# A second plain unit for expert 0, other places for two sets of weight maxima, and a reordered opening in a fused AdaLN, scan and mixture-of-experts kernel

## The reference, cut to what matters

```python
mod = (silu(c) @ wmod).reshape(4, 6, 1, 512)          # six rows of 512 for each batch
sa, ca, ga, sb, cb, gb = (mod[:, i] for i in range(6)) # ga, gb kept away from 0
h = layernorm(x) * (1 + ca) + sa
xn = rmsnorm(h) * gamma
q, kv, a = split(xn @ w_qkva.T)                        # 512 columns each
s[t] = sigmoid(a[t]) * s[t - 1] + kv[t]                # a scan over the tokens
x = x + ga * (q * s)
h = layernorm(x) * (1 + cb) + sb
p = softmax(h @ Wr); the two best experts of each token; at most 320 rows per expert and batch
y = relu(rows @ W1[e] + b1[e]) @ W2[e] + b2[e]
x = x + gb * (sum over the two experts of p * y)
```

## Time and profile before

| what | us |
|---|---|
| median of 3 runs | 2270.05 (2268.99 to 2272.29) |
| the profiled execution, its time | 2275.81 |
| its span, first to last instruction | 2274.0 |
| PE busy | 2172.6 (96%) |
| DVE busy | 1634.9 (72%) |
| ACT busy | 1042.0 (46%) |

### The profile page before, as it was taken

One profiled execution on the slowest core, in us unless ns is written; L12 is line 12 of the kernel. 1 busy time (PEld: TensorE's weight loads), 2 busy tenths in 40 slices (PEclk: granted clock), 3 DMA queues, 4 the chain that ended last, 5 costly groups with the idle time before them and its releaser, 6 DMA issues.

```text
span 2274.0 us, 34385 instructions
## 1 busy us (share of the span) xinstructions
PE 2172.6 (96%) x12890; PEld 1194.3 (53%) x12890; DVE 1634.9 (72%) x2864; ACT 1042.0 (46%) x2051; POOL 362.8 (16%) x334
## 2 busy tenths in 40 slices
PE   4899999999996889999999999999999999999997
PEld 1345455555463455564646556465555646556463
DVE  6398898898785778758758775875876687587441
ACT  4256676575443254434615534362552535255150
POOL 1014334334232101000010110101011010100101
PEclk7999999999998999999999999999999999999999
DMA  7759999576663534533544453454445355343201
GB/s 239 221 160 240 234 257 204 140 194 135 145 191 79 153 116 125 147 79 94 143 115 100 128 146 76 113 143 95 121 107 140 84 116 145 88 116 94 42 6 24
DMA packets 353064, 300.99 MB, mean 132 GB/s; under 512 B 242459, under 2 KB 242459, under 8 KB 352384
## 3 DMA queue, kind: packets, MB, share of 16 engines
q1 hardware_dynamic: 331136, 256.63, 41.2%
q0 software_dynamic: 21760, 42.14, 9.9%
HBM read 163.84 MB, written 93.01 MB: 113 GB/s over the span
## 4 chain that ended last, share of the span: by engine, by line
PE 86%; DVE 5%; DMA 3%; issue 2%; SPq 2%; ACT 1%; POOL 0%; another core or an unknown queue 0%; DVEq 0%; POOLq 0%; ACTq 0%
PE bank L1964 34%; PE bank L1907 28%; PE bank L1819 20%; DMA reg_d<-in_w 2%; PE bank L1896 1%; PE bank L1774 1%; PE bank L1741 1%; PE bank L1785 1%; DMA reg_e<-reg_e 1%; SPq L484 1%; SPq L476 1%; DVE wm L1481 0%; PE bank L1734 0%; DMA reg_d<-in_wmod 0%; DVE reg_e L1522 0%
## 5 line engine op out<-in xcount | busy, mean ns | idle before, releaser
L1964 PE MATMUL bank<-reg_b,reg_c 128*128 128x512 f16 x3840 | 833.6, 379 | 18.2 <-DVE reg_e L1442 17.2
L1964 PEld LDWEIGHTS bank<-reg_b,reg_c 128*128 128x128 f16 x3840 | 375.8, 98 | 470.8 <-DVE reg_e L1442 18.6
L1819 PE MATMUL bank<-reg_c 128*128 128x512 f16 x2304 | 511.4, 381 | 11.5 <-DMA reg_c<-reg_a 11.5
L1907 PE MATMUL bank<-reg_e,reg_a 128*128 128x320 f16 x2880 | 450.2, 300 | 8.1 <-DVE reg_e L1513 4.5
L1819 PEld LDWEIGHTS bank<-reg_c 128*128 128x128 f16 x2304 | 223.7, 98 | 274.9 <-issue 20.1
L1907 PEld LDWEIGHTS bank<-reg_e,reg_a 128*128 128x128 f16 x2880 | 281.7, 98 | 122.8 <-DVE reg_e L1513 4.8
L731 POOL DMA_INDIRECT out_dram<-reg_e,midx x80 | 139.9, 1749 | 1044.1 <-DVE reg_e L1446 933.0
L940 ACT ACTIVATE reg_e<-bank,b1s 128x320 f32<-128x320 f32 x120 | 63.2, 527 | 410.0 <-PE bank L1907 410.0
L1907 PE MATMUL bank<-reg_e,reg_d 128*128 128x320 f16 x1440 | 234.7, 301 | 8.2 <-DVE reg_e L1536 8.2
L1442 DVE SCALAR_TENSOR_TENSOR reg_e<-bank,inv,reg_e 128x512 f32<-128x512 f32 x80 | 59.8, 748 | 241.8 <-PE bank L1964 241.8
L1907 PEld LDWEIGHTS bank<-reg_e,reg_d 128*128 128x128 f16 x1440 | 140.3, 98 | 68.0 <-DVE reg_e L1536 9.2
(11 more groups left out here) (227 smaller groups left out, 2600.3 us busy)
## 6 DMA issues: line engine op xcount, KB each, us to landing
reg_d<-in_w SPq DMA_DIRECT2D x232, 512.0 KB, 4.4
slot_rows<-zrow SPq DMA_DIRECT2D x32, 516.0 KB, 5.1
reg_b<-in_x SPq DMA_DIRECT2D x16, 1024.0 KB, 7.6
out_dram<-reg_b SPq DMA_DIRECT2D x16, 1024.0 KB, 7.3
reg_d<-in_w SPq DMA_DIRECT2D x8, 1024.0 KB, 8.8
slot_rows<-zrow SPq DMA_DIRECT2D x32, 129.0 KB, 5.0
reg_d<-in_wmod SPq DMA_DIRECT2D x4, 1024.0 KB, 14.4
reg_e<-mod_rows SPq DMA_DIRECT2D x7, 512.0 KB, 9.6
```

Source lines behind the costliest of these rows:

```text
L1819: ins = mm(dst[:, :], wqs[:, ws, kc, e0:e0 + P], xns[:, j % 2, xs, kc, :], start=kc == 0 and xs == 0 and ws == 0, stop=kc == KC - 1 and ws ...
L1907: ins = mm(dst[:, 0:CAP], w[ws][:, c, p * P:(p + 1) * P], xs_of[:, KC * xs + 2 * i + c, j * CAP:(j + 1) * CAP], start=first and c == 0 and ...
L1964: ins = mm(bank_y[i % 2][:, :], hid[:, hs, hc, t * P:(t + 1) * P], w2s[:, ws, hc, :], start=k == 0 and hs == 0 and ws == 0, stop=k == HC - ...
```

## The change

1. **Unit 1 is plain too** (`PLAIN = 2`). `first_unit` becomes `plain_unit(u)` and runs for v = 0 and 1; pairs are counted from unit 2 on (`pairs_to`). The sums of expert 0 on DVE and ACT, their eight fills, and `x_sums`, `x_hi`, `x_lo` of unit 1 are gone.
2. **Maxima of expert 1.** The fills of its `w1` for the maxima stand first in the order of the fills, the first four of them ahead of SP's wait for the scattered rows. DVE takes the eight maxima of `w1` at t = 0 and t = 3 of unit 0's outputs, and those of `w2` in the plain unit 1, after every third lo part from i = 6 on. POOL's `all_max(1, 0)` moves to tile 3 of unit 0.
3. **Opening.** `wmod` piece 1 is loaded and spread ahead of piece 0. PE makes all six batch rows ahead of the first attention product, row 5 in bank 1. DVE takes two of the four maxima of `wq` between the two halves of `apply1`. SP issues the transposes of block 0 before the loads of blocks 2 and 3. The loads of expert 0's `w1` move behind the transposes of block 1, and its maxima to the end of step 1 and the middle of step 2, with their scale.

```diff
-MOD_BANK = {0: 6, 1: 5, 2: 2, 3: 3, 4: 4, 5: 5}
+MOD_BANK = {0: 6, 1: 5, 2: 2, 3: 3, 4: 4, 5: 1}
+MOD_DONE = {1: 1, 0: 2, 2: 5, 3: 6, 4: 7, 5: 8}
...
+        def pairs_to(v):
+            return NP * (v - PLAIN)
...
# sync
+            load_wmod(1)
             load_wmod(0)
-            load_wmod(1)
...
-            sp.wait_ge(s_modmm, 5)
-            load_x(0, 2)
...
             turn_x(0, 0)
+            sp.wait_ge(s_modmm, MOD_DONE[5])
+            load_x(0, 2)
+            load_x(0, 3)
...
                 if has(i, 1):
                     turn_x(*rel(q, j, 1))
+                if i == 0:
+                    for c in range(4):
+                        sp.dma_start(stage[:, c, :], w1[0, c * P:(c + 1) * P, :]).then_inc(s_stg[c], 16)
+                    sp.dma_start(b1r[:, :], b1[0, :, :]).then_inc(s_b1, 16)
...
                 load_gb()
+                bring_w1(1, fill_max(1, 0), 0)
                 for k in range(2):
                     sp.wait_ge(s_send[k], 16 * 2 * TB * NB // 2)
                 sp.wait_ge(s_xt, 16)
                 load_unit(1, 1)
-                bring_w1(0, fill_w1(0), 0)
-                bring_w1(0, fill_w1(0), 1)
...
# scalar
             square(0)
             hi1(0)
+            mod_copy(0)
+            mod_copy(1)
             act.wait_ge(s_wch0, WQ_LINKS - 4)
...
-                    if u == 0 and e == 0:
-                        sums_hi(0, 0)
-                    if v + 1 < 2 * E:
+                    if PLAIN <= v + 1 < 2 * E:
                         x_hi(v + 1)
...
# vector
             apply1(0, 0, 0)
+            wq_max(0)
+            wq_max(1)
+            apply1(0, 0, 1)
+            wq_max(2)
+            wq_max(3)
...
                 if i == 1:
                     scales_done()
-                    for c in (0, 1):
+                if i == 2:
+                    for c in (2, 3):
                         w_max_quarter(0, 0, c)
                     w_scale_head(0, 0)
...
-                    for c in (2, 3):
+                if i == 1:
+                    for c in (0, 1):
                         w_max_quarter(0, 0, c)
...
+                    elif i >= W2_NEXT and i % 3 == 0 and (i - W2_NEXT) // 3 < 8:
+                        max_piece(1, 1, (i - W2_NEXT) // 3)
...
                 if u == 0 and e == 0:
                     if t == 0:
-                        sums(0, 0)
...
                         for k in range(4):
                             max_piece(1, 0, k)
+                    if t == 3:
+                        for k in range(4, 8):
+                            max_piece(1, 0, k)
+                        scale_head(1, 0)
+                    if t == 4:
+                        scale_tail(1, 0)
...
# tensor
+            mod_spread(1)
             mod_spread(0)
-            mod_spread(1)
+            mod_mm(0)
+            mod_mm(1)
...
-            for m in range(2, 5):
+            for m in range(2, 6):
+                if m == 5:
+                    pe.wait_ge(s_modc, 1)
                 mod_mm(m)
...
-                if n == 0 and c == 0 and kind == 2:
-                    pe.wait_ge(s_modc2, 3)
+                if n == 0 and c == 0 and kind == 1:
+                    pe.wait_ge(s_modc2, 6)
...
             for v in range(2 * E):
-                if v == 0:
-                    first_unit()
+                if v < PLAIN:
+                    plain_unit(v)
```

More of the change, by code:

```diff
@@ L63 @@
 NLINK = 12
+PLAIN = 2
+W2_NEXT = 6
 EXPONENT = 0x7F800000
@@ L572, in next_unit @@
             def next_unit(v):
-                wait(sp, s_p3, NP * (v - 1))
+                if v == PLAIN:
+                    sp.wait_ge(s_mm1, 2 * HC * PLAIN)
+                wait(sp, s_p3, pairs_to(v))
                 wait_alone(sp, s_meta, v - 1)
@@ L867, in step @@
                     sigmoid(n, 2)
-                    if i == 0:
-                        for m in (5, 0, 1):
-                            mod_copy(m)
                     sigmoid(n, 3)
@@ L919, in first_unit @@
                     hb, b = i // 2, i % 2
-                    wait(act, s_mm1, i + 1)
-                    wait(act, s_hlo, i + 1)
-                    bias = b1s[:, b, hb:hb + 1]
+                    wait(act, s_mm1, 2 * HC * u + i + 1)
+                    wait(act, s_hlo, 2 * HC * u + i + 1)
+                    bias = b1s[:, 2 * u + b, hb:hb + 1]
                     src = bank_h[i % 4][:, 0:CAP]
@@ L985, in blocks_hi @@
             def blocks_hi(e, f):
-                wait(act, s_p3, NP * (2 * e - 1))
+                if 2 * e == PLAIN:
+                    act.wait_ge(s_mm1, 2 * HC * PLAIN)
+                wait(act, s_p3, pairs_to(2 * e))
                 wait(act, s_nch, NLINK * (e - 1) + 7)
@@ L1151, in _, with wq_max @@
             apply1(0, 0, 0)
-            apply1(0, 0, 1)
-            for c in range(KC):
+            def wq_max(c):
                 dve.wait_ge(s_wqraw[c], 16)
@@ L1409, in b1_scale @@
             def b1_scale(e):
-                wait(dve, s_h21, NP * (2 * e - 1))
+                if e > 0 and 2 * e == PLAIN:
+                    dve.wait_ge(s_hhi, 2 * HC * PLAIN + 4)
+                wait(dve, s_h21, pairs_to(2 * e))
                 for b in range(B):
@@ L1589, in x_sums @@
                 wait(dve, s_xt, 16 * (v + 1))
-                wait(dve, s_p3, NP * (v - 1))
-                wait(dve, s_l12, NP * (v - 1))
+                if v == PLAIN:
+                    dve.wait_ge(s_hlo, 2 * HC * PLAIN + 4)
+                wait(dve, s_p3, pairs_to(v))
+                wait(dve, s_l12, pairs_to(v))
                 v_.tensor_tensor(x32[:, :, :], x_raw[:, 0:KC, :], x_raw[:, KC:2 * KC, :], ALU.add).then_inc(s_x32, 1)
@@ L1918, in pair_step @@
                     wait(pe, s_h21, n - 2)
-                    if p % 4 == 0 and (v == 1 or v % 2 == 0):
+                    if n == 0:
+                        pe.wait_ge(s_hhi, 2 * HC * PLAIN + 4)
+                    if p % 4 == 0 and v % 2 == 0:
                         for q in range(4):
```

166 lines of the change are left out of this document (66 added, 100 removed).

## The result

The changed kernel takes 2210.98 us, the median of 4 runs (2210.73 to 2212.34), against 2270.36 us (2268.99 to 2272.29) of the kernel before: 59.4 us less, a ratio of 0.9739 with a 95% interval of 0.9722 to 0.9756. The forecast was 2210.5.

A forecast was written before the change was run, and what follows sets the result against it. PE bounds the kernel, busy 96% of the span, so gains lie in its idle time, lower clock or less work. Units 34.8 plus opening 24.8 give 59.6 us: 2270.05 - 59.6 = 2210.5 us, range 2203 to 2222.

The forecast's parts named there:

- Unit 0's second layer: Experts: with earlier fills, PE's 16.45 us wait before the third tile goes; the layer ends at 750.9.
- The cover: Unit 0's second layer: tile 0 is free near 713, PE needs it at 719.8, so 7 us of lateness cost nothing.
- The 8.8 us of landing: Unit 0's first four fills: time from first issue to the end of the DMA wait, so they land at about 706.1.
- Unit 1's first layer: Experts: 384 matmuls at 0.1358 us take 52.2 us against 68.0, no wait; second layer starts 34.8 us sooner.
- The rivals in the units: Fills pace unit 1: 2226 us, chance 0.07; clock drops in plain unit: 2215, 0.04; unit 2 starves: 2282, 0.02.
- Opening: Up to the first attention product: PE starts it at 47.2 instead of 59.16, bounds 44 and 50.
- Step 1: Starts at 82.4 instead of 105.1, held by block 1's transposes behind the zero fills; takes 33.0 us instead of 41.0.
- My 11.5: Block 1's transposes before step 1: time from first issue until the last was needed and there, in the kernel before.
- Steps 2 and 3: Attention steps that receive the moved maxima, 4.48 us twice: 77 us together instead of 71.1, bounds 70 and 80.1.
- everything hidden: Lower bound of steps 2 and 3, 70 us; as a rival, DVE hides the moved maxima: 2200 us, chance 0.11.
- the 5.20 us wait: Kernel before: PE's wait for DVE at step 1's start, with 4.48 us of maxima ahead of it on DVE.
- The base: Time the 59.6 us gain is taken from: the median 2270.05 us, not the profiled 2275.81; profiled span expected near 2214.

The follow-up runs named there:

- the eighth experiment: Changed kernel with eight more maxima of the same four quarters, 9.2 us of DVE, ahead of unit 0's first output: 2212.60 us.
- the fourth experiment: Changed kernel with the first four fills of expert 1's w1 put back behind the wait for scattered rows and the load of unit 1's rows: 2226.77 us.
- the third: Kernel before with only the first four w1 fills for the sums moved ahead of SP's wait for scattered rows; unit 1 keeps seven products: 2261.55 us.
- the second kernel: Kernel before with only the opening changed, including the moved maxima of expert 0's w1; units as before: 2245.77 us.

## Why the prediction was right

**Unit 0's second layer**: no wait at tile 2, 722.33 - 669.19 = 53.1 us, forecast 53.2 (697.7 to 750.9). The cover was 8.1 us by the eighth experiment, where 7 were forecast. The 8.8 us of landing are those of all four fills; the first was there after 4.8 in the fourth experiment. Under that cover it made no difference.

**Unit 1's first layer**: 52.2 us from start to start, forecast 52.2, and no wait for a fill. Of the 105.3 us between the second layers (forecast 105.4) the gain is 34.9, forecast 34.8. What I could not have said is how it divides; the third and fourth experiments do. My text gave the tile's wait to the place of the fills alone, but with the seven-product form that place brings less than half of what the layer lost, since the rows of unit 1 are next.

**The rivals in the units** fell: no fill paced unit 1, the granted clock was 1.00 over unit 1's first layer, its upper level of 2.4 GHz (the row below is that stretch: us, busy time and count of PE, PEld, DVE, ACT and POOL, clock, DMA share, GB/s), and unit 2 started behind unit 1's second layer with no gap, at 826.29. The Trainium skill ("TensorE: Matmul & The Clock Gate", section "A second HAM failure mode: psum-queue depth-cycling") tells of a PE that idles briefly between groups of matmuls as it goes round its banks, and so drops in and out of the lower clock. This stretch does not show it: 384 matmuls over four banks kept a pitch of 0.136 us with no idle time between them.

```profile
722.00:775.00 53.00, 53.00 (x390) 37.94 (x388) 25.37 (x43) 27.20 (x62) 1.55 (x1) 1.00 0.28 85
```

**Opening**: first product at 47.65, forecast 47.2; its terms were off in part. The four batch rows behind the maxima started at 31.56 as told, but the lower clock cost them 9.29 - 7.03 = 2.3 us, not 1.2. That price is no constant: the nine traces with this opening have from 0 to 2.5 us at this place, and the first product at 44.9 to 48.6.

Step 1 began at 81.85, forecast 82.4, with 2.24 us of wait, forecast 3.3. This term was right by luck, since two errors cancelled. The zero fills went out at 57.36, not 55.0, and the transposes at 73.58, not 71.1; but they landed 8.3 us later, not 11.3. My 11.5 (which went into the sum as 11.3) was no landing time: PE did not wait at 105.1, so the rows of before show only that the transposes were there by then. Step 1 took 114.7 - 81.85 = 32.8 us, forecast 33.0. Steps 2 and 3 took 192.1 - 114.7 = 77.4, forecast 77. In all 216.8 - 192.1 = 24.7, forecast 24.8. So close a match is chance too: with the same code, step 4 began at 214.8 to 216.8 in three traces of the old opening, and at 189.7 to 192.1 in four of the new.

**Steps 2 and 3**: with everything hidden I put them at 70, and the experiments with short and with spread maxima took 69.3 and 68.8. Between the profiled executions the 8.96 us of moved maxima cost 77.4 - 69.3 = 8.1 us, through 2.77 + 0.35 + 0.86 + 1.40 us of wait and the lower clock; between the medians they cost 6.9 us, where I charged 7. The forecast of 77 was a choice near the upper bound, by likeness to the 5.20 us wait, and not a sum of waits.

**The base**: the gain was taken from the median, not from the profiled execution, whose 2275.81 us would have given 2216. The execution shown of before had a slow first layer of unit 0 that the change does not touch. For the same reason the profiled span came out at 2210.6 us and not near 2214, as I had expected.

## What to carry to other kernels

A wait inside a chain of engines has a second-latest cause, and the gain of an edit is the distance to it: the same four fills moved forward brought 8.6 us in one form of the next layer and 15.5 in the other. A simpler form with more matmuls can win where the clever one needs prepared operands at a bad moment: 48 more matmuls, 6.5 us, went against 16.6 us of waits and some 5.8 us of lower clock (51.4 - 336 x 0.1358) in that layer, and the fills' place paid in full. Work that must move is put where its engine has slack in every step, piece by piece, not ahead of the result that PE waits for.

## What the runs showed of the hardware

The lower clock's price does not follow the length of the wait alone. Behind 2.77 us of wait, 8 transposes and 12 matmuls took 5.7 us in one execution and 6.9 in another, against 3.8 undisturbed. In the opening, behind waits of 2.74 and 0.70 us, 16 f32 matmuls took 9.29 us in the changed kernel, 8.73 in the fourth and 9.57 in the second, and in the eighth, with a granted clock of 1.00, 7.03; the code up to there is the same. Behind 1.40 and behind 0.97 us there was none to be seen. Behind 12.66 us it was 2.9 us over 144 matmuls, and in the second kernel, behind 16.61 us, 33.30 - 31.1 = 2.2.

A maximum over 128x1024 lasts 1.21 to 1.22 us in all 112 cases of the changed kernel. Eight in a row took 9.10 us, so one started every (9.10 - 1.21) / 7 = 1.13 us, a little before the last had ended.
